# Attention with a token-mixing FFN on one core: VectorE and the DMAs transpose one tile of each pair in query rows 2 and 3 too

## The reference, cut to what matters

```python
x = L0_attn_x                      # (8, 1024, 256), float32
xn = layernorm(x)
# attention: 8 query heads of 128, one shared key/value head of 128
q = (xn @ Wq + bq) -> (8, 8, 1024, 128);  k, v = split(xn @ Wkv + bkv)
q = q + pe;  k = k + pe            # sinusoidal positions
scores = q @ k.T / sqrt(128), causal
attn = softmax(scores) @ v;  a = concat_heads(attn) @ Wo
# FFN: mixes each token with the one before it
xr, xk = mu_r*xn + (1-mu_r)*x_prev, mu_k*xn + (1-mu_k)*x_prev
f = sigmoid(xr @ W_r.T) * (square(relu(xk @ W_k.T)) @ W_v.T)
out = x + a + f
```

## Time and profile before

| | |
|---|---|
| time, median of 3 runs (lowest to highest) | 1561.39 us (1560.83 to 1561.88) |
| the profiled execution: its own time | 1561.37 us |
| its span, first to last instruction | 1559.6 us |
| TensorE busy | 1533.5 us, 98% |
| DVE / ACT / POOL busy | 1210.4 / 1056.2 / 1060.7 us |
| TensorE transposes of score squares (L986) | 1472 |
| mean granted TensorE clock | 0.996 of full speed |

### The profile page before, as it was taken

The page is one execution under the profiler, slowest core; times in us unless marked ns, Lnnn a source line. Parts: engine busy times, 40 slices in busy tenths (PEclk is TensorE's granted clock), DMA queues, the critical chain, the costliest instruction groups (busy, mean ns, idle before and its releaser), DMA issues.

```text
span 1559.6 us, 35317 instructions
## 1 busy us (share of the span) xinstructions
PE 1533.5 (98%) x12032; PEld 1497.6 (96%) x12032; DVE 1210.4 (78%) x3284; ACT 1056.2 (68%) x2531; POOL 1060.7 (68%) x1549
## 2 busy tenths in 40 slices
PE   5999999999999999999999999999999999999998
PEld 5999999999999999999999999999999999999998
DVE  6888767887678876788768787688876888768875
ACT  5776667766667766677577676676766677666764
POOL 5666776667756777567775676756766577765765
PEclk8999999999999999999999999999999999999999
DMA  4014420244202441024410244103431034300443
GB/s 139 9 53 121 146 75 22 58 122 148 69 15 69 129 143 55 15 75 134 144 42 15 86 141 127 42 15 98 140 129 32 12 112 138 129 20 8 119 147 105
DMA packets 151425, 132.46 MB, mean 85 GB/s; under 512 B 12240, under 2 KB 146512, under 8 KB 151248
## 3 DMA queue, kind: packets, MB, share of 16 engines
q1 hardware_dynamic: 150672, 129.55, 27.0%
q10 hardware_dynamic: 576, 0.66, 0.1%
HBM read 67.25 MB, written 62.91 MB: 83 GB/s over the span
## 4 chain that ended last, share of the span: by engine, by line
PE 76%; POOL 10%; issue 7%; DVE 5%; ACT 1%; DMA 0%; POOLq 0%; DVEq 0%; ACTq 0%
PE pS L893 25%; PE pO L893 23%; PE pG L893 19%; PE pT L986 8%; POOL qt L450 3%; POOL X L506 3%; DVE gate L698 1%; POOL pt L465 1%; POOL mh L456 1%; DVE X L872 1%; POOL rstd L434 1%; DVE mix L742 1%; POOL v L444 1%; POOL X L505 1%; DVE pt L797 1%
## 5 line engine op out<-in xcount | busy, mean ns | idle before, releaser
L893 PE MATMUL pO<-pt,v 128*128 128x256 f32 x3456 | 466.6, 285 | 6.5 <-DVE ot L848 5.3
L893 PE MATMUL pS<-kt,qt 128*128 128x288 f32 (+41 forms) x2304 | 458.6, 329 | 2.0 <-POOL qt L450 2.0
L659 ACT ACTIVATE X<-X,bias 128x16 f32<-128x16 f32 (+56 forms) x512 | 375.9, 734 | 93.3 <-DVE bias L872 92.8
L893 PEld LDWEIGHTS pO<-pt,v 128*128 128x128 f32 x3456 | 426.1, 189 | 12.1 <-DVE ot L848 10.0
L872 DVE CUSTOM_DVE_ANT_0 X<-pS,mask 128x16 f32<-128x16 f32 (+56 forms) x512 | 353.8, 691 | 45.1 <-issue 22.9
L506 POOL TENSOR_SCALAR X<-X,rec 128x16 f32<-128x16 f32 (+56 forms) x512 | 367.0, 717 | 23.0 <-DVE rec L780 23.0
L893 PEld LDWEIGHTS pS<-kt,qt 128*128 128x128 f32 x2304 | 367.5, 190 | 14.0 <-issue 2.2
L465 POOL TENSOR_TENSOR pt<-Z,pt 128x640 fp32r<-128x640 f32 (+3 forms) x128 | 256.6, 2005 | 63.3 <-ACT pt L588 61.6
L797 DVE TENSOR_TENSOR pt<-pT,pt 128x512 fp32r<-128x512 f32 (+3 forms) x512 | 257.3, 522 | 26.6 <-ACT pt L595 23.7
L595 ACT CAST pt<-pT 128x512 fp32r<-128x512 f32 (+3 forms) x512 | 223.0, 461 | 61.7 <-PE pT L986 58.8
L652 ACT CAST ot<-pO 128x256 fp32r<-128x256 f32 x256 | 96.2, 376 | 241.2 <-PE pO L893 115.0
(11 more groups left out here) (101 smaller groups left out, 1788.6 us busy)
## 6 DMA issues: line engine op xcount, KB each, us to landing
park_dram<-Y SPq DMA_DIRECT2D x32, 512.0 KB, 2.6
Z<-park_dram SPq DMA_DIRECT2D x128, 128.0 KB, 2.8
park_dram<-Y SPq DMA_DIRECT2D x32, 448.0 KB, 3.0
Z<-park_dram SPq DMA_DIRECT2D x128, 112.0 KB, 2.5
park_dram<-Y SPq DMA_DIRECT2D x32, 384.0 KB, 2.9
Z<-park_dram SPq DMA_DIRECT2D x128, 96.0 KB, 2.3
park_dram<-Y SPq DMA_DIRECT2D x32, 320.0 KB, 2.7
Z<-park_dram SPq DMA_DIRECT2D x128, 80.0 KB, 2.1
```

What stands on the lines that cost most here:

```text
L659: nc.scalar.activation(x_row(s, 0, w), x_row(s, 0, w), ACT.Exp, bias=bias[:, j:j + 1], scale=-1.0, accum_out=total[:, j:j + 1]).then_inc(e ...
L893: last = nc.tensor.matmul(out, a[i], m[j], start=start and k == 0, stop=stop and k == n - 1)
```

## The change: what it does

- `turned(s)` now holds from s = 16 on: the even steps of rows 2 and 3 go by DVE, DRAM, ACT and POOL as those of rows 4 to 7 do.
- `Z` is gone. The fetched squares land in the low-part buffer `pt[1]`, which now has three pair slots; ACT casts from there to `pt[0]`, and POOL subtracts in place. `Y` has two slots and `park_d` four. SP's `move` is split into `park` (turn s+3) and `fetch` (turn s+4); a fetch waits until the pair three back has been multiplied. Park and fetch now stand ahead of that turn's stores and reloads on SP.
- Both `pt` buffers change their layout from key tile by 256 query columns to (step, 32-row block, key tile, 32 columns). The product with V reads its moving operand as 8 runs of 32 columns rather than one run of 256.
- `HALVES` covers all 64 steps with ten half buffers; a step's mask waits for the transpose of whichever turned step used its halves before.
- `xnt` and `xt` have one slot rather than two; ACT waits, before it overwrites them, for the work that read them.
- On TensorE, WO stands ahead of the other products and of the product with V. On DVE the norm and mixing parts stand behind the evacuations of the turn, on POOL the Q and V splits ahead of the mixing ones. `TURNS`, `WO_AT`, `AT` move some entries; `LEAD` is 10 rather than 12. Weights are staged elsewhere, and DVE clears both `pT` banks at the start.
- `scaled_by_act(s)` is never true (s > 999), so the code under it does nothing.

```diff
-H_LAG = 7
-L_LAG = 7
+H_LAG = (7, 6)
+L_LAG = (7, 7)
+PT_SLOTS = (2, 3)
-LEAD = 12
+LEAD = 10
@@ TURNS, chunk 0
-     (12, "KV", 1, 0),
+     (11, "KV", 1, 0),
-     (15, "KT", 1, 0)),
+     (14, "KT", 1, 0)),
@@ TURNS, chunk 1
-     (11, "Q", 1, 2),
-     (12, "FV", 0, 0),
-     (12, "KV", 1, 0),
+     (9, "Q", 1, 2),
+     (11, "KV", 1, 0),
      (12, "Q", 1, 3),
-     (14, "KT", 1, 0)),
+     (13, "KT", 1, 0),
+     (14, "FV", 0, 0)),
@@ TURNS, chunk 2: FV 12 -> 14, KT 13 -> 12; chunk 3: FR 5 -> 7
-WO_AT = (17, 25, 33, 41, 49, 57, 66, 72)
+WO_AT = (17, 26, 33, 41, 49, 56, 65, 73)
-      "mixr_prev": (0, 1, 0, 0),
-      "mixr_dve": (1, 1, 1, 1),
+      "mixr_prev": (0, 0, 0, 0),
+      "mixr_dve": (0, 1, 1, 0),
-      "ka_out": (6, 5, 6, 8),
-      "mixk_prev": (5, 7, 6, 7),
-      "mixk_dve": (6, 13, 9, 11),
-      "mixk_out": (8, 14, 13, 13)}
+      "ka_out": (8, 5, 6, 8),
+      "mixk_prev": (5, 4, 6, 7),
+      "mixk_dve": (9, 12, 11, 10),
+      "mixk_out": (10, 14, 14, 13)}
...
 def turned(s):
-    return s >= SHARED and s % 2 == 0
+    return s >= 16 and s % 2 == 0
...
-        Y = sb("Y", [P, 4, NT, 32])
-        Z = sb("Z", [P, 2, 4, NT, 32])
-        pt = [sb(f"pt{i}", [P, 2, NT, 2 * P], R) for i in range(2)]
+        Y = sb("Y", [P, 2, 4, NT, 32])
+        pt = [sb(f"pt{i}", [P, PT_SLOTS[i], 2, 4, NT, 32], R) for i in range(2)]
...
+            def park(b, s):
+                k, nk = turned_no(b, s), s // H + 1
+                sp.wait_ge(turned_ready, k + 1)
+                if k >= 4:
+                    sp.wait_ge(landed[k % 4], 64 * (k // 4))
+                sp.dma_start(park_d[k % 4, :, :, 0:nk * 32],
+                             Y[:, k % 2, :, 0:nk, :].rearrange("p a k c -> p a (k c)")).then_inc(parked[k % 2], 16)
+            def fetch(b, s):
+                k, nk = turned_no(b, s), s // H + 1
+                sp.wait_ge(parked[k % 2], 16 * (k // 2 + 1))
+                pair = b * (STEPS // 2) + s // 2
+                if pair >= PT_SLOTS[1]:
+                    sp.wait_ge(pv_done, pair - PT_SLOTS[1] + 1)
+                to = pt_of(1, b, s).bitcast(F)
                 for q in range(4):
...
+                if it - V_LAG - 1 in TURNED:
+                    fetch(b, it - V_LAG - 1)
+                if it - V_LAG in TURNED:
+                    park(b, it - V_LAG)
...
+                    nc.gpsimd.tensor_tensor(pt_of(1, b, s)[:, :, 0:nk, :], pt_of(1, b, s)[:, :, 0:nk, :].bitcast(F),
+                                            pt_of(0, b, s)[:, :, 0:nk, :].bitcast(F), ALU.subtract).then_inc(turned_lo, 1)
...
+                if n:
+                    act.wait_ge(xt_ready, n)
+                    act.wait_ge(prev_ready, 2 * n * CT)
+                    act.wait_ge(mix_ready, 2 * n * CT)
...
-                        last = product(pO[:, 0:2 * P], [([x[:, k, :] for x in v], [x[:, pair % 2, k, :] for x in pt])],
+                        high, low = [x[:, (b * (STEPS // 2) + pair) % n, :, :, k, :].rearrange("p i a c -> p (i a) c")
+                                     for x, n in zip(pt, PT_SLOTS)]
+                        last = product(pO[:, 0:2 * P], [([x[:, k, :] for x in v], [high, low])],
                                        start=k == 0, stop=k == nk - 1)
```

More of the change, by code:

```diff
@@ L102, in halves_of, with zeroed, turned_before, scaled_by_act @@
 def halves_of(s):
-    if s < SHARED:
-        return HALVES[s], 1
-    return (s // 2 % 2 * 2, 2) if turned(s) else ((s - SHARED) // 2 % 3 * 2 + 4, 2)
+    return HALVES[s], 1 if s < SHARED else 2
 def turned(s):
-    return s >= SHARED and s % 2 == 0
+    return s >= 16 and s % 2 == 0
+def zeroed(s):
+    return P - (s % H + 1) * SUB
+def turned_before(s):
+    j, n = halves_of(s)
+    found = []
+    for half in range(j, j + n):
+        back = 1
+        while not halves_of((s - back) % STEPS)[0] <= half < sum(halves_of((s - back) % STEPS)):
+            back += 1
+        if turned((s - back) % STEPS):
+            found.append((TURNED.index((s - back) % STEPS), s < back))
+    return found
+def scaled_by_act(s):
+    return s > 999
 def width(s):
@@ L138, in absent, with t_banks @@
     return c == NC and b == B - 1
+def t_banks(s):
+    n = s // H + 1
+    return [] if turned(s) else [(k, min(4, n - k)) for k in range(0, n, 4)]
 def users_before():
@@ L144, in users_before @@
     for b, it in turns():
+        if it >= T_LAG and it - T_LAG < STEPS:
+            order += [(b, ("T", it - T_LAG, m)) for m in range(len(t_banks(it - T_LAG)))]
         order += [(b, u) for u in FILL[it] if not absent(b, u[1])]
@@ L149, in users_before @@
     for b, u in order:
-        bank = u[1] % 2 + 1 if u[0] == "S" else G_BANK.get(u, 0)
+        if u[0] == "S":
+            bank = u[1] % 2 + 1
+        elif u[0] == "T":
+            bank = 3 + (T_FIRST[u[1]] + u[2]) % 2
+        else:
+            bank = G_BANK.get(u, 0)
         before[b, u] = last.get(bank)
@@ L153, in users_before @@
     return before
-BEFORE = users_before()
-def t_banks(s):
-    n = s // H + 1
-    return [] if turned(s) else [(k, min(4, n - k)) for k in range(0, n, 4)]
 T_FIRST = [sum(len(t_banks(r)) for r in range(s)) for s in range(STEPS + 1)]
 T_BODY = T_FIRST[STEPS]
-N_FIRST = [sum(1 if r % H == H - 1 else 2 for r in range(s)) for s in range(STEPS + 1)]
+N_FIRST = [sum((zeroed(r) > 0) + (not scaled_by_act(r)) for r in range(s)) for s in range(STEPS + 1)]
 N_BODY = N_FIRST[STEPS]
 TURNED = [s for s in range(STEPS) if turned(s)]
+C_FIRST = [sum(1 for r in range(s) if scaled_by_act(r)) for s in range(STEPS + 1)]
+BEFORE = users_before()
 def build(nc, x_d, wq_d, wkv_d, wo_d, wr_d, wk_d, wv_d, bq_d, bkv_d, mu_d, pet_d, petok_d, out_d, park_d):
@@ L215, in build @@
         half = sb("half", [P, TPC])
-        xnt = sb("xnt", [P, 2, CT, CHUNK + 1])
-        xt = [sb(f"xt{i}", [P, 2, CT, CHUNK], R) for i in range(2)]
+        xnt = sb("xnt", [P, CT, CHUNK + 1])
+        xt = [sb(f"xt{i}", [P, CT, CHUNK], R) for i in range(2)]
         qt = [sb(f"qt{i}", [P, 2, CHUNK // SUB, H, SUB], R) for i in range(2)]
@@ L293, in build @@
         turned_ready = sem("turned_ready")
-        parked = sem("parked")
-        landed = [sem(f"landed{i}") for i in range(2)]
+        parked = [sem(f"parked{i}") for i in range(2)]
+        landed = [sem(f"landed{i}") for i in range(4)]
+        scaled = sem("scaled")
         turned_hi = sem("turned_hi")
@@ L470, in turn @@
                     if kind == "XT":
-                        split_xt(chunk_no(b, c), c % 2)
+                        split_xt(chunk_no(b, c))
+                for kind, c, p in FILL[it - 2] if it > 1 else []:
+                    if absent(b, c):
+                        continue
+                    if kind == "Q":
+                        split_q(chunk_no(b, c), c % 2, p, 1)
+                for kind, c, p in FILL[it - 1] if it else []:
+                    if absent(b, c):
+                        continue
+                    if kind == "Q":
+                        split_q(chunk_no(b, c), c % 2, p, 0)
+                    elif kind == "KV" and c < NC:
+                        split_v(chunk_no(b, c), c)
                 c, i = it // PER, it % PER
@@ L580, in turn @@
             def turn(b, it):
-                s = it - H_LAG
-                if s in TURNED:
+                for s in [s for s in TURNED if s + H_LAG[s % 2] == it]:
                     nk = s // H + 1
@@ L643, in turn @@
                                              ACT.Tanh, scale=0.5).then_inc(tanh_ready, 1)
+                s = it - C_LAG
+                if 0 <= s < STEPS and scaled_by_act(s):
+                    w = width(s)
+                    j = halves_of(s)[0]
+                    act.wait_ge(rec_ready, b * STEPS + s + 1)
+                    nc.scalar.activation(x_row(s, 0, w), x_row(s, 0, w), ACT.Copy, scale=rec[:, j:j + 1]
+                                         ).then_inc(scaled, 1)
                 first = it - PV_LAG - 1
@@ L863, in turn @@
                         o = x_row(s, 0, w).rearrange("p (a n) -> p a n", a=2)
-                    if turned(s):
-                        left = b * len(TURNED) + TURNED.index(s) - 1
-                    else:
-                        left = b * len(TURNED) - (s < 2) if s < SHARED else 0
-                    if left > 0:
-                        dve.wait_ge(turned_ready, left)
+                    for k, earlier in turned_before(s):
+                        if b >= earlier:
+                            dve.wait_ge(turned_ready, (b - earlier) * len(TURNED) + k + 1)
                     dve.wait_ge(s_filled, b * STEPS + s + 1)
```

205 lines of the change are left out of this document (94 added, 111 removed).

## The result

The changed kernel takes 1566.09 us (median of 11 runs, 1564.44 to 1567.25), the one before 1561.69 us (11 runs, 1560.65 to 1562.36): a ratio of 1.0029, with an interval from 1.0019 to 1.0038. It is slower by about 4.5 us. Forecast was 1541 us, in a range from 1531 to 1555.

The account below looks back on a forecast made before the run. TensorE, busy 1533.5 of 1559.6 us, was taken as the bound: 1559.6 - 24.6 for squares + 4 for waits = 1539 us of span, 1540.8 with 1.8 us around it, so 1541; range 1531 to 1555.

Parts of the forecast that it names:

- together 0.5 us a batch, 4 us: Timetables, order and buffers: all new waits add 4 us, with 0.2 us a batch for late masks.
- room on average: POOL in rows 2 to 4: 9.8 us a batch of new subtractions fit idle 5.0, 10.9 and 7.2 us.
- nothing in sum: DVE transposes and ACT casts of the new turned steps: they cost about what the work they replace did.
- each moved product has its input two turns or more behind it: TensorE's moved KV, KT, FV, WO: no waits, but for WO at turn 56, 0 to 0.4 us, taken as nothing.
- own signs of failing: TensorE: idle time growing over 1 us a batch, or busy time falling by much else than 24.6 us.
- The mask that was to come late in row 6: Chunks 0 and 3's mixing before a mask: up to 1.3 us late, with a short TensorE wait in row 6.
- the changed read of TensorE: 3456 products with V reading 8 runs of 32 columns: 0 to 11 ns a matmul, 0 to 39 us, taken as 0.
- The price of a square: TensorE, rows 2 and 3: each square removed saves 0.11 us of the chain, 24.6 us in all.
- The late square of step 16: Row 2: ACT waits 1.6 us for step 16's fetched squares before its cast, and TensorE 0.3 us for `ot`.
- The run-wise read costs: Rival: TensorE's read in runs costs 11 ns a matmul, 1580 us; decides from 6 ns; 0.10 with the other slower rival.
- Late squares: Rival, chance 0.18: ACT's 1.6 us wait passes on in full each batch, late masks cost half: 1549 us.
- GpSimd blocks VectorE: Rival: 64 new POOL subtractions each hold DVE and TensorE for their length, 1619 us; 0.10 with the other slower rival.

Follow-up runs that it names:

- e7: The changed kernel without turning steps 28 and 30, half buffers given out anew: 1558.77 us, ratio 0.9983 to the kernel before.
- e8: The changed kernel without turning step 24: 1559.91 us, ratio 0.9994 to the kernel before.
- e2: The changed kernel with steps turned from row 4 on only, half buffers as before: 1567.32 us, ratio 1.0032 to the kernel before.
- e6: The changed kernel without turning row 3's steps (row 2 and rows 4 to 7 turned), half buffers reassigned: 1557.38 us, ratio 0.9975 to the kernel before.
- e1: The kernel before with only the new layout of the two probability buffers: 1571.22 us against 1562.45, ratio 1.0053.
- e5: The changed kernel with the old layout of the probability buffers and `Z` back with two slots: 1560.49 us, ratio 0.9996 to the kernel before.
- e10: The changed kernel with old layout and `Z`, steps 28 and 30 not turned, WO behind the product with V: 1550.52 us, ratio 0.9929 to the kernel before.
- e3: The kernel before with only turned steps from row 2 on and the half buffers they need: 1594.74 us, ratio 1.0208.
- e12: The changed kernel with old layout, old timetables, two slots of `Y`, park and fetch apart, WO late: 1592.67 us, ratio 1.0202 to the kernel before.
- e9: The changed kernel with VectorE's transpose of a turned step behind the evacuations of its turn: 1591.59 us, ratio 1.0188 to the kernel before.

## Why the prediction was wrong, by its own steps

**The steps that failed.** First, the term "together 0.5 us a batch, 4 us" for all waits. Behind it stood "room on average" for GpSimd, "nothing in sum" for VectorE and ScalarE, both read over whole rows, and a search for late squares in row 2 only. The waits came at the start of row 4, at the one bank that products share from turn 32 on. What counts there is what stands ahead of two evacuations in their queues: for L877 two transposes of 0.69 us and a norm that GpSimd's subtraction of step 26 makes 1.0 us longer, for `ka` a late mask of VectorE. I had asked only whether "each moved product has its input two turns or more behind it"; the WO and XT of turns 33 and 34 were not moved at all, and they wait for their *bank*. It cost 12.0 + 3.3 us on the matmuls' rows. e7 shows it for L877 (without steps 28 and 30, no such wait), e8 for `ka`, e2 and e6 for both. The prediction's own signs of failing came true: TensorE's idle time grew by 15.1 us, 1.9 us a batch where 1 was the limit, and its busy time is 1524.3 us rather than 1509. The mask that was to come late in row 6 was no part of it: TensorE waited for a mask once, 0.4 us.

Second, the changed read of TensorE, taken as 0 between bounds of 0 and 39 us: it is 8.8 us alone (e1), 5 to 8 in the changed kernel (e5; e10 against e7, where WO's place changed too). The bounds held; the choice between them was wrong. The price of 0 that was also drawn there from the Trainium skill, "SBUF — State Buffer" (Door 1: The DMA port swizzle), does not hold for this operand: runs of 128 bytes cost it 3.0 to 3.2 ns a matmul.

**The sum with what was measured**, on the profiled runs: -24.6 (squares) + 10.4 (3456 products * 3.0 ns) + 15.1 (idle time) + 5 (left over) = +5.9 us. Most of what is left over are waits too. The records of matmuls overlap (285 ns long, 118 ns apart), so the first 0.17 us of a wait count as busy. From start to start, behind the first 60 us, whatever exceeds the usual distance by over 30 ns adds up to 19.3 us before and 38.7 us in the change: +19.4 us, where the idle time there shows +15.3.

**What held.** The price of a square: row 2 gave 8.9 of 10.6 us. The instructions' sizes:

```profile
L499 POOL TENSOR_TENSOR pt<-pt 128x512 fp32r<-128x512 f32 x32 | 44.8, 1401 | 1.0
...
L499 POOL TENSOR_TENSOR pt<-pt 128x384 fp32r<-128x384 f32 x32 | 32.8, 1026 | 16.7 <-ACT pt L626 16.5
...
L837 DVE STREAM_TRANSPOSE Y<-X 128x512 f32<-128x512 f32 x32 | 22.1, 692 | 5.9 <-POOL X L541 5.9
...
L837 DVE STREAM_TRANSPOSE Y<-X 128x384 f32<-128x384 f32 x32 | 18.3, 573 | 13.3 <-POOL X L541 13.3
```

That is 1.40 and 1.03 us for 1.35 and 1.09, and 0.69 and 0.57 for 0.70 and 0.57. The late square of step 16 is there too, smaller: ScalarE waited 0.91 us for it, and 0.77 us for step 18's, which I had called early.

```profile
1220.29 0.52 ACT L626 CAST pt<-pt 128x384 fp32r<-128x384 f32 x1 [0.91 <-DMA pt<-park_dram]
...
1224.88 0.52 ACT L626 CAST pt<-pt 128x384 fp32r<-128x384 f32 x1 [0.77 <-DMA pt<-park_dram]
```

TensorE did not wait for `ot` behind it.

**The rivals.** "The run-wise read costs" had the right mechanism at half of its deciding price; it needed the waits to turn the sign. The measured sign, slower, was given a chance of 0.10, and not by this sum of two causes. "Late squares" named ScalarE in row 2, not the bank in row 4. "GpSimd blocks VectorE" is seen (norm 915 ns rather than 792). By the readings of e6 and e7 it takes 1.0 us, most of the room ahead of XT, and the transposes then make the wait: neither does it alone. The transposes' part is shown by e7; the change without the hold was not run. Nor were the -4 us of e2 against e1 taken apart by timetable, order and buffers.

## What to carry to other kernels

When work moves off the engine that bounds a kernel, don't ask whether the others have room on average in that stage: for each buffer that the bounding engine refills, list what is queued ahead of the instruction that frees it, there and a stage later. Then take the part of the move that has room: the first four steps of eight gave 8.9 us, the other four took it back. A layout chosen for a transfer is paid by each reader, as often as it reads; here 3 ns 3456 times was over a third of the gain.

## What the runs showed of the hardware

- A moving operand of 256 float32-sized columns in 8 runs of 32 rather than in one costs TensorE 3.0 to 3.2 ns a matmul (118.4 to 121.4 and 121.6 ns from start to start, at a mean granted clock of 0.996 to 0.998). As an estimate from that clock, 2.4 GHz, seven jumps between runs at one column time of 0.42 ns would be 2.9 ns.
- TensorE's granted clock fell where it idled longer: in e3, busy for 1.47 of 3.60 us, it was then granted 1.2 rather than 2.4 GHz. Over e12's six runs a mean granted clock of 0.987 rather than 0.996 goes with 15.9 us.
- A chain of transpose, park, fetch, cast has little room: moving its first instruction behind one or two evacuations of some 0.4 to 0.9 us each cost 25 us (e9 against the change, 1.0188 and 1.0029).
